# First attention stage: the transposes of the next rows go one slot later, the weights are split in two pieces, and three waits of the first batch move

## The reference, cut to what matters

```
def _L0_attn_ref(x, Wq, Wk, Wv, Wo, bo):     # H = 16 heads of 64
    q = (x @ Wq).reshape(b, n, H, DH)
    k = (x @ Wk).reshape(b, n, H, DH)
    v = (x @ Wv).reshape(b, n, H, DH)
    scores = einsum('bihd,bjhd->bhij', q, k) * scale + slope * (pos_i - pos_j)
    scores = where(causal, scores, -1e30)
    attn = softmax(scores)
    return einsum('bhij,bjhd->bihd', attn, v).reshape(b, n, H * DH) @ Wo + bo

x = x + _L0_attn_ref(_layernorm(x), ...)
x = x + _L0_xattn_ref(_layernorm(x), ...)    # five more stages follow
```

## Time and profile before

| what | us |
|---|---|
| median of 3 runs | 1642.35 |
| lowest and highest | 1638.7, 1642.84 |
| the profiled execution | 1642.86 |
| its span | 1641.1 |
| busy in the span: PE | 1477.3 (90%) |
| DVE | 1103.3 (67%) |
| ACT | 1014.1 (62%) |
| POOL | 497.3 (30%) |

### The profile page before, as it was taken

One profiled execution on the slowest core, in us unless ns is written; L12 is line 12 of the kernel. 1 busy time (PEld: TensorE's weight loads), 2 busy tenths in 40 slices (PEclk: granted clock), 3 DMA queues, 4 the chain that ended last, 5 costly groups with the idle time before them and its releaser, 6 DMA issues. The chain is left out here.

```text
span 1641.1 us, 39731 instructions
## 1 busy us (share of the span) xinstructions
PE 1477.3 (90%) x11703; PEld 1127.0 (69%) x11751; DVE 1103.3 (67%) x3548; ACT 1014.1 (62%) x2723; POOL 497.3 (30%) x828
## 2 busy tenths in 40 slices
PE   6999999999999878779999968999989968997798
PEld 4777777777777656458888845565556537775597
DVE  5777677776777558756666637778877745772565
ACT  5777677776777546266666636666666645662354
POOL 4333233332333235123333222333223105531133
PEclk9999999999999988779999979999999989996999
DMA  6000000000000040001111110000000000000000
GB/s 209 2 0 0 0 0 0 0 0 0 0 0 0 2 167 26 14 15 44 45 42 45 37 51 14 14 13 11 8 13 13 6 1 1 2 2 1 1 26 26
DMA packets 34079, 34.77 MB, mean 21 GB/s; under 512 B 5601, under 2 KB 29793, under 8 KB 33249
## 3 DMA queue, kind: packets, MB, share of 16 engines
q1 hardware_dynamic: 29664, 25.07, 4.7%
q0 software_dynamic: 4352, 8.92, 2.2%
HBM read 25.07 MB, written 8.91 MB: 21 GB/s over the span
## 5 line engine op out<-in xcount | busy, mean ns | idle before, releaser
L596 POOL TENSOR_SCALAR a_prob<-a_prob,a_inv 128x128 f32<-128x128 f32 (+1 forms) x256 | 126.6, 504 | 359.8 <-DVE a_inv L496 359.8
L430 ACT ACTIVATE a_prob<-a_psS,a_low 128x128 f32<-128x128 f32 (+1 forms) x512 | 210.0, 436 | 0.0
L486 DVE CUSTOM_DVE_ANT_0 a_psS<-a_psS,a_bias 128x128 f32<-128x128 f32 (+1 forms) x512 | 167.9, 390 | 45.7 <-PE a_psS L308 32.0
L1784 ACT ACTIVATE a_probT<-a_psZ 128x512 f32<-128x512 f32 x256 | 138.9, 594 | 75.4 <-PE a_psZ L1570 75.4
L421 ACT COPY a_probT<-a_psT 128x384 f32<-128x384 f32 x256 | 123.5, 482 | 95.3 <-PE a_psT L352 93.9
L1867 DVE TENSOR_REDUCE a_low<-a_psS 128x4 f32<-128x1024 f32 x128 | 156.7, 1224 | 26.4 <-PE a_psS L1570 25.3
L352 PE MATMUL a_psT<-ident,a_prob 128*128 128x128 f32 x768 | 138.8, 290 | 2.9 <-ACT a_probT L421 2.8
L1311 POOL DMA_INDIRECT d_rows<-rows_dram,source x72 | 68.2, 947 | 193.6 <-PE e_psX L1393 143.9
L308 PE MATMUL a_psS<-a_qk 64*128 64x128 f32 (+1 forms) x1024 | 120.4, 354 | 1.7 <-ACT a_qk L413 0.7
L352 PEld LDWEIGHTS a_psT<-ident,a_prob 128*128 128x128 f32 x768 | 80.2, 141 | 54.2 <-issue 46.4
L430 ACT ACTIVATION_READ_ACCUMULATOR a_prob<-a_psS,a_low 128x1 f32 x512 | 113.3, 221 | 0.0
(11 more groups left out here) (359 smaller groups left out, 4198.6 us busy)
## 6 DMA issues: line engine op xcount, KB each, us to landing
sorted_out<-e_y SPq DMA_DIRECT2D x72, 64.0 KB, 1.6
in_lo<-in_gate_up SPq DMA_DIRECT2D x4, 1024.0 KB, 6.9
x<-in_x SPq DMA_DIRECT2D x8, 256.0 KB, 6.9
down<-in_down SPq DMA_DIRECT2D x1, 2048.0 KB, 15.1
rows_dram<-rows SPq DMA_DIRECT2D x8, 256.0 KB, 2.2
out<-x SPq DMA_DIRECT2D x8, 256.0 KB, 2.3
d_rows<-rows_dram,source POOLq DMA_INDIRECT x72, 2.7
a_sel_in<-in_sel SPq DMA_DIRECT2D x1, 1024.0 KB, 4.8
```

Of the source, the lines that this page charges most:

```text
L430: nc.scalar.activation(prob[:, 2 * (p % 4) + k, lo:hi], psS[:, u, lo:hi], ACT.Exp, bias=low[:, u, i:i + 1], scale=-1.0, accum_out=total[:, ...
L486: nc.vector.tensor_tensor_reduce(psS[:, u, lo:hi], psS[:, u, lo:hi], bias0[:, 2 * p + k, lo:hi], 1.0, LEAST, ALU.add, ALU.min, low[:, u, i ...
L596: nc.gpsimd.tensor_scalar(w, w, inv[:, 2 * (q % 2) + 1, i:i + 1], 1.0, ALU.mult, ALU.mult).then_inc(norm_done[1], 1)
L1784: nc.scalar.activation(probT[:, (p + half + 1) % 2, 2 * half + c, :, :].rearrange("p j s -> p (j s)"), psZ[:, c, :], ACT.Exp, scale=-1.0). ...
```

## The change

It makes four edits, all in `layer0_attention`.

1. The weights are rounded and split in two pieces: the first 256 columns of wq, wk and wv, then the other 768 of each. ACT's `keep_a(0, 0)` stands between the two groups. PE's first `project` waits for two pieces only (wq and wk, first columns), the V matmuls of slot 0 for the third, and the `project` of pair 2 (called in slot 1) for all six.
2. PE's wait for wo moves from the start to `output(1)`; DVE's wait for bo and for the loads of x moves from before slot 0 to slot 4 of the first batch.
3. POOL copies `a_cur_lo` of the first batch after four of the 16 instructions of the bias table, where it stood behind all of them.
4. The transposes of the next batch's rows (`ln_in.turn`), with their wait for the V copy of slot 5, go from the end of slot 5 to slot 6, behind the scores.

```diff
@@ PE
                 ln_in.turn(pe, 0, psM)
-                pe.wait_ge(w_split, 3)
-                pe.wait_ge(loaded["wo"], 16)
                 project(0, 0)
...
                     pe.wait_ge(next_split, b + 1)
+                if isinstance(b, int) and b == 0 and p == 0:
+                    pe.wait_ge(w_split, 2)
+                elif isinstance(b, int) and b == 0 and p == 2:
+                    pe.wait_ge(w_split, 6)
...
                     pe.wait_ge(cur_lo_ready, b + 1)
+                if isinstance(b, int) and b == 0 and p == 0:
+                    pe.wait_ge(w_split, 3)
...
                     if new:
                         scores(b, p, has_unit)
+                    if p == 6 and prep:
+                        pe.wait_ge(v_kept, b * PAIRS + 6)
+                        ln_in.turn(pe, b + 1, psM)
...
-                    if p == 5 and prep:
-                        pe.wait_ge(v_kept, b * PAIRS + 6)
-                        ln_in.turn(pe, b + 1, psM)
@@ ACT
-                    nc.scalar.activation(w_hi[:, k, :], w_in[k][:], ...
+                    round_weights(k, W_HEAD)
                 keep_a(0, 0)
+                for k in range(3):
+                    round_weights(k, W_REST)
@@ DVE
-                for k in range(3):
-                    dve.wait_ge(w_rounded, k + 1)
-                    nc.vector.scalar_tensor_tensor(out=w_lo[:, k, :], ...
-                dve.wait_ge(loaded["bo"], 16)
-                for sem in x_in[1:]:
-                    dve.wait_ge(sem, 16)
+                for n, at in enumerate((W_HEAD, W_REST)):
+                    for k in range(3):
+                        dve.wait_ge(w_rounded, 3 * n + k + 1)
+                        nc.vector.scalar_tensor_tensor(out=w_lo[:, k, at], ...
...
                 for p in range(PAIRS):
+                    if isinstance(b, int) and b == 0 and p == 4:
+                        dve.wait_ge(loaded["bo"], 16)
+                        for sem in x_in[1:]:
+                            dve.wait_ge(sem, 16)
@@ POOL
                 for h in range(H):
+                    if h == 4:
+                        rest_for_values(0)
                     nc.gpsimd.tensor_scalar(bias0[:, h, :], ...
```

More of the change, by code:

```diff
@@ L256, in layer0_attention @@
         blocks = [(0, 0, P), (1, P, 3 * P)]
+        W_HEAD, W_REST = slice(0, S), slice(S, H * DH0)
         @block.sync
@@ L357, in output @@
                 pe.wait_ge(o_kept, b * PAIRS)
+                if isinstance(b, int) and b == 1:
+                    pe.wait_ge(loaded["wo"], 16)
                 for i in range(BT):
@@ L468, in first, with round_weights @@
                     act.wait_ge(loaded[name], 16)
-                    nc.scalar.activation(w_hi[:, k, :], w_in[k][:], ACT.Copy, scale=1.0 if k else -(DH0 ** -0.5)).then_inc(w_rounded, 1)
+                    round_weights(k, W_HEAD)
                 keep_a(0, 0)
+                for k in range(3):
+                    round_weights(k, W_REST)
+            def round_weights(k, at):
+                nc.scalar.activation(w_hi[:, k, at], w_in[k][:, at], ACT.Copy, scale=1.0 if k else -(DH0 ** -0.5)).then_inc(w_rounded, 1)
             rounds_ahead(act, first, slots)
@@ L566, in first @@
                 split_next(0)
-                for k in range(3):
-                    dve.wait_ge(w_rounded, k + 1)
-                    nc.vector.scalar_tensor_tensor(out=w_lo[:, k, :], in0=w_in[k][:], scalar=1.0 if k else -(DH0 ** -0.5),
-                                                   in1=w_hi[:, k, :].bitcast(F32), op0=ALU.mult, op1=ALU.subtract).then_inc(w_split, 1)
-                dve.wait_ge(loaded["bo"], 16)
-                for sem in x_in[1:]:
-                    dve.wait_ge(sem, 16)
+                for n, at in enumerate((W_HEAD, W_REST)):
+                    for k in range(3):
+                        dve.wait_ge(w_rounded, 3 * n + k + 1)
+                        nc.vector.scalar_tensor_tensor(out=w_lo[:, k, at], in0=w_in[k][:, at], scalar=1.0 if k else -(DH0 ** -0.5),
+                                                       in1=w_hi[:, k, at].bitcast(F32), op0=ALU.mult, op1=ALU.subtract).then_inc(w_split, 1)
             rounds_ahead(dve, first, slots)
@@ L586, in first, with rest_for_values @@
                 for h in range(H):
+                    if h == 4:
+                        rest_for_values(0)
                     nc.gpsimd.tensor_scalar(bias0[:, h, :], dist[:], float(SLOPES0[h]), 1.0, ALU.mult, ALU.mult).then_inc(bias_set, 1)
+            def rest_for_values(b):
+                pool.wait_ge(next_split, b + 1)
+                if not (isinstance(b, int) and b == 0):
+                    pool.wait_ge(v_done, b * PAIRS)
+                pool.sem_inc(pool_seen, 1)
+                nc.gpsimd.tensor_copy(cur_lo[:], next_lo[:].bitcast(F32)).then_inc(cur_lo_ready, 1)
             def norm(b, p):
@@ L599, in slots @@
                 for p in range(PAIRS):
[L600 to L605, removed]
+                    if new and p == 0 and has_unit(p, 8):
+                        rest_for_values(b)
                     if has_unit(p, 1):
```

## The result

| | before | changed |
|---|---|---|
| median, us | 1642.59 (4 runs, 1638.7 to 1642.87) | 1631.89 (4 runs, 1630.01 to 1634.4) |
| ratio | | 0.9941, 95% interval 0.9921 to 0.9961 |
| the same kernel timed again on another occasion | 1641.93 (21 runs) | 1632.42 (5 runs), ratio 0.9948, 0.9935 to 0.9962 |
| span of the profiled execution | 1641.1 | 1632.6 |
| end of the first attention in the profile | 579.24 | 571.86 |

The account below looks back on a forecast made before the run. PE, busy 90% of the span, was taken as the bound, with start holes and V copy waits. From the profiled 1642.86, 6.5 for the start and 0 for edit 4 gave 1636.4 (1635.9 from the median); range 1631.5 to 1639.7.

Parts of the forecast that it names:

- First project at 9.4: At the start, PE's first project needs only 256-column pieces and begins at 9.4 instead of 13.40, 4.0 us earlier.
- Scores of slot 1 at 15.7, of slot 2 at 19.6: First batch: slot 1 scores start at 15.7 against 22.08, 6.4 us earlier; slot 2 scores follow at 19.6.
- Its 3.91 us stay: Slot 1 of the first batch keeps its length of 3.91 us (22.08 to 25.99) if nothing is late.
- The cap of 6.4 to 7.1: Slot 2's second transposes need POOL's norm, behind the whole bias table, so the start gains at most 6.4 to 7.1 us.
- 4.0 us for the pieces and 2.4 for the hole in front of V: Split of the 6.4 us gain at slot 1's scores: 4.0 from weight pieces, 2.4 from PE's hole before V.
- Edit 4 is worth 0: In later batches, the 7.7 us of V copy waits return as 14 waits of some 0.6 us for a_next_lo.
- Both gains: Rival: the moved transposes also keep 14 x 0.55 = 7.7 us on top of the start, 1628.2 us; chance 0.07.
- The clock eats the gain: Rival: PE's clock still rises at 26.6, leaving a 3.7 us gain, 1638.7; chance 0.13 shared with the port case.
- The shared port eats it: Rival: six DVE pieces delay POOL's bias table 2.6 us, gain 3.8 or more, about 1638.5; 0.13 with clock case.
- Nothing: Rival: the start gains nothing because a load covered the first batch, 1642 us; chance 0.05.
- slower: Rival: later transposes make ACT's copy hold keep_t of slot 6, up to 0.85 us a batch, 1648.7; chance 0.04.
- the leading case: Only the start of the first attention gains, 6.5 us; own range 1633.5 to 1638, chance 0.71.

Follow-up runs that it names:

- second profile: The changed kernel, unchanged, timed and profiled again beside the kernel before: 1632.42 against 1641.93 us, ratio 0.9948.
- the table put later: Changed kernel with POOL beginning the bias table only after the rests of the first two pieces: 1636.08 us against 1641.93 for the kernel before, ratio 0.9959.
- the start alone: Changed kernel with the row transposes back in slot 5, edits 1 to 3 kept: 1652.42 us against 1663.24 for the kernel before, ratio 0.9942.
- the early rest: Changed kernel with DVE making a_next_lo in slot 6, ahead of the V copy: 1653.66 us against 1663.24 for the kernel before, ratio 0.9951.
- the pieces alone: Kernel before with edit 1 only, weights in two pieces and PE's wait for wo moved: 1638.78 against 1641.08 us, ratio 0.9989.
- the copy alone: Kernel before with edit 3 only, a_cur_lo copied after four bias instructions: 1639.00 us, ratio 0.9990.
- the transposes alone: Kernel before with edit 4 only, the next rows' transposes moved to slot 6: 1661.83 against 1663.24 us, ratio 0.9993.

## Why the prediction was right, point by point

**First project at 9.4.** 9.79 in the first profile, 9.34 in the second. The piece was taken at 0.43 us; it is 0.42 us alone and 0.72 us beside the bias instructions. The price of that contention stood in the prediction, but on the wrong edge of the two: it was charged to POOL's table, not to DVE's first pieces. The table with the copy took 11.7 us (8.27 to 19.94) against 12.1 before, no longer.

**Scores of slot 1 at 15.7, of slot 2 at 19.6.** 16.00 and 19.45 (15.54 and 18.59 in the second profile). The walk from the first project was right within 0.1 us. "Its 3.91 us stay" was the mis-sized step: 3.45 us, and 3.05 in the second profile, because the clock rose in slot 1. The prediction named this as likely and left it out of the 6.5.

**The cap of 6.4 to 7.1.** The mechanism exists: in the second profile, and with the table put later, PE waits 0.59 and 0.58 us for `norm`, at a gain of 6.96 and 6.81 us by the scores of slot 3. But it is no fixed cap. It was worked out with the load of the distances at 8.88 us; where that load came at 8.25 and 8.29 us, `norm` was over by 20.9 and the gain was 7.32 and 7.35 us (the start alone and the early rest), beyond 7.1. In the first profile of the changed kernel the table held nobody. All these gains are against the one profile of the kernel before, the latest of four with its start; against their mean the changed start gains 6.4 us. So 6.5 was as good as these runs can tell, and its closeness is in part luck, since the early rise and the slower pieces, both outside the sum, worked against each other.

**The terms.** The prediction counted 4.0 us for the pieces and 2.4 for the hole in front of V. The sum of both held (6.08 us at slot 1), the split did not mean what it seems to: the pieces alone leave 0.84 us or less at slot 3, the copy alone 4.5 in one profile (2 by the total), and the moved wait for x, to which the prediction gave no share, is worth 4.35 us with both and nothing without the pieces. It is one chain with three gates.

**Edit 4 is worth 0.** Right, with its mechanism: 7.4 us of waits for `a_next_lo` in 14 places, 0.52 us where 0.6 was said, and at most 0.4 to 0.6 us kept in all. The end of the chain was put too early. It is not `a_next_lo` but the V copy of slot 7, as the kernel with the early rest showed; for edit 4 both give the same answer, for the early rest they did not, and 7 us were expected of it that did not come.

**The rivals.** Both gains: refuted by the transposes alone (ratio 0.9993, the wait for `a_next_lo` in place of the other) and by the start alone. The clock eats the gain: the opposite happened. The shared port eats it: 0.3 us for each of two pieces in the first profile, nothing in the second, and nothing on POOL's table. Nothing, and slower: not seen; ACT's copy of the rows held nobody.

**The total.** The first attention gives 7.4 us in the pair of profiles, 0.9 more than the sum, and less against the other profiles of the old start. The medians gave 10.7 and 9.5, the ratios 9.7 and 8.5. The rest, 1 to 3 us, is inside both intervals and of the size by which two profiles of one program differ behind this stage; that a part of it is a lasting effect on the later stages is not excluded. The median of 1631.89 lies outside the range of the leading case (1633.5 to 1638) and only 0.4 us inside the whole range, whose lower end was put at 1631.5 for a double gain that did not happen. That the range held owes something to luck: nothing in the sum stands for these 1 to 3 us.

## What to carry to other kernels

A wait that one engine shows for another names the result, not the bound: before moving the waiting instruction, ask whether the releasing engine was busy up to it without a break of its own to spare. Where it was, the wait came back at another place, once when the waiting engine's order changed and once when the releasing engine's did, and what paid was work taken out of the releasing engine's chain; a hole in that engine just ahead of the chain is the place to put it. At a program's start the gates stand in series: time them together, and look for the next gate, because removing one alone may pay next to nothing. And take the start from several profiles before a gain below a microsecond is read from it.

## What the runs showed of the hardware

- A DVE weight rest of 256 columns with two inputs in SBUF takes 0.42 us alone and 0.72 us beside POOL's bias instructions; one of 768 columns takes 0.96 to 1.26 us.
- A hole in PE near the start can cost more than its length where the clock has just risen: after 2.75 us of standing the scores were back at 1.65 us. In the five profiles with all of edits 1 to 3 the rise came in slot 1 (between 16.0 and 18.4 us).
- With the same start the clock rose at different places: the scores of slot 3 came at 28.18 to 29.30 us in four profiles whose first project began within 0.15 us, and in one of them the clock rose, fell and rose again (scores of 1.00 us, a project row of 0.58, scores of 1.34).
- Two profiles of one program differed by 4.0 us in one stretch of 570 matmuls, with a granted clock of 0.80 and 0.82.
- The load of the distances landed at 8.27 and at 8.88 us in two runs of one program, enough to decide which engine meets which.
- The kernel before took 1663 us on one chip and 1641 and 1642 us on two others; the first attention, with this start, ended at 578.0 and 578.6 us in profiles on the first and at 579.2 us elsewhere.
